# A gated attention block with a split-FP32 feed-forward: sum transfers, token loads and weight splits of chunk 0 at other places

## The reference

```python
x = x + tanh(g_xattn[0]) * wkv(time_decay, time_first, layernorm(x), ctx_2048)   # x is 16 x 256 x 512
x = x + tanh(g_ffn[0]) * ffn(layernorm(x), W1, W2, W3)

# ffn: D = 512, H = 2048
hidden = silu(x @ W1.T) * (x @ W3.T)
hidden = fwht(hidden)            # Walsh-Hadamard over H, normalised by 1/sqrt(H)
out = hidden @ W2.T
```

## Time and profile before

| | us |
|---|---|
| runs of the kernel | 1056.58 (median), 1054.04, 1057.97 |
| profiled execution | 1057.62 |
| its span, first to last instruction | 1055.8 |
| tensor engine busy | 997.6 (94%) |
| VectorE busy | 801.8 (76%) |
| ScalarE busy | 439.6 (42%) |
| GpSimd busy | 274.2 (26%) |
| first pair of chunk 1 starts at | 216.07 |
| mean granted clock of the tensor engine | 0.988 |

### The profile page before, as it was taken

One profiled execution on the slowest core, in us unless ns is written; L12 is line 12 of the kernel. 1 busy time (PEld: TensorE's weight loads), 2 busy tenths in 40 slices (PEclk: granted clock), 3 DMA queues, 4 the chain that ended last, 5 costly groups with the idle time before them and its releaser, 6 DMA issues.

```text
span 1055.8 us, 17503 instructions
## 1 busy us (share of the span) xinstructions
PE 997.6 (94%) x6988; PEld 691.6 (66%) x6988; DVE 801.8 (76%) x1288; ACT 439.6 (42%) x736; POOL 274.2 (26%) x212
## 2 busy tenths in 40 slices
PE   5799899689999999999999999999999999999998
PEld 4565344256677677776777777777777777777775
DVE  7977594989989995889769995889669994753334
ACT  6875342246243443455243542444243542522221
POOL 1344232211432033211422124221322124211111
PEclk9999999799999999999999999999999999999999
DMA  9699999694885446354745446353645433444331
GB/s 352 233 340 291 321 255 227 109 355 168 293 301 173 151 188 240 100 213 155 267 164 178 146 177 239 114 218 143 264 160 180 163 126 151 160 166 165 125 145 41
DMA packets 47042, 210.03 MB, mean 199 GB/s; under 512 B 9328, under 2 KB 26864, under 8 KB 36336
## 3 DMA queue, kind: packets, MB, share of 16 engines
q1 hardware_dynamic: 38128, 192.13, 50.2%
q0 software_dynamic: 8832, 16.78, 7.6%
HBM read 183.70 MB, written 41.97 MB: 214 GB/s over the span
## 4 chain that ended last, share of the span: by engine, by line
PE 69%; DVE 17%; DMA 6%; issue 5%; ACT 2%; SPq 0%; DVEq 0%; POOL 0%
PE pl L714 8%; PE pl L716 8%; PE pl L715 8%; PE po L726 7%; PE po L728 7%; PE pg L714 6%; PE pg L715 6%; PE pg L716 6%; PE po L737 4%; PE po L735 4%; DMA bv<-x_tok 2%; DMA wts<-up_stage 2%; DVE x L1432 2%; DVE work L1604 2%; DVE bv L1295 1%
## 5 line engine op out<-in xcount | busy, mean ns | idle before, releaser
L1759 POOL TENSOR_TENSOR work<-work 128x512 bf16<-128x512 f32 x112 | 163.9, 1464 | 595.4 <-DVE work L1604 595.4
L726 PE MATMUL po<-work,w 128*128 128x512 f16 x456 | 173.0, 379 | 2.2 <-DVE x L1432 1.3
L728 PE MATMUL po<-work,w 128*128 128x512 f16 x456 | 172.8, 379 | 0.0
L1060 ACT ACTIVATE work<-work 128x256 f32<-128x256 f32 x168 | 68.4, 415 | 210.2 <-DVE work L1511 210.1
L714 PE MATMUL pg<-wts 128*128 128x256 f16 x448 | 122.5, 273 | 4.8 <-DVE work L1511 4.7
L1511 DVE TENSOR_TENSOR work<-pl,wts 128x256 f32<-128x256 f32 x168 | 65.1, 414 | 80.1 <-PE pl L716 77.5
L715 PE MATMUL pg<-wts 128*128 128x256 bf16 x448 | 122.4, 273 | 0.0
L716 PE MATMUL pg<-wts 128*128 128x256 f16 x448 | 122.4, 273 | 0.0
L714 PE MATMUL pl<-xn,wts 128*128 128x256 f16 x448 | 122.3, 273 | 0.0
L715 PE MATMUL pl<-xn,wts 128*128 128x256 bf16 x448 | 122.2, 273 | 0.0
L716 PE MATMUL pl<-xn,wts 128*128 128x256 f16 x448 | 122.1, 273 | 0.0
(11 more groups left out here) (206 smaller groups left out, 2159.6 us busy)
## 6 DMA issues: line engine op xcount, KB each, us to landing
wts<-up_stage SPq DMA_DIRECT2D x56, 2048.0 KB, 8.0
up_stage<-wts SPq DMA_DIRECT2D x8, 1024.0 KB, 13.2
up_stage<-wts SPq DMA_DIRECT2D x16, 512.0 KB, 8.2
ev<-ctx_t SPq DMA_DIRECT2D x7, 1024.0 KB, 11.0
xin<-x_t SPq DMA_DIRECT2D x7, 1024.0 KB, 7.5
bv<-x_tok SPq DMA_DIRECT2D x7, 1024.0 KB, 10.0
out_t<-x SPq DMA_DIRECT2D x7, 1024.0 KB, 4.8
wts<-up_sums SPq DMA_DIRECT2D x11, 512.0 KB, 9.0
```

The source lines that it names most:

```text
L726: pe.matmul(po[:, d, :], w2h[:, j, d * P:d * P + P], hh[:, b, :], start=start, stop=False, skip_group_check=True)
L728: pe.matmul(po[:, d, :], w2l[:, j, d * P:d * P + P], hh[:, b, :], start=False, stop=False, skip_group_check=True)
L1060: act.activation(sg[:, slot, cols], src, ACT.Silu, scale=(1.0, -1.0)[slot]).then_inc(acted, 1)
L1759: pool.tensor_tensor(hl[:, b, :], hf[:, slot, :], hh[:, b, :], ALU.subtract).then_inc(pair_lo, 1)
```

## The change

Four things move; no instruction's work is changed and none is added or taken away.

1. GpSimd's list between W2's tiles: the first adds of group 0 and the copies of group 1 are issued behind the clamp of tile 7 instead of behind that of tile 10 and the first two low halves; the second adds of group 0 and the first adds of group 1 come in front of the clamps of tiles 11 and 12; the third adds of group 0 behind the clamp of tile 15. `STEPS_AT` places the rest, in slots 0 to 9 instead of 0 to 12.
2. Units 14 and 15 are cast and split in slots 4 and 5 instead of 12 (`unit_slot`).
3. `SUMS_AT`: sums 0 and 1 both in slot 5, 2 in slot 8, 3 and 4 in slot 10, 5 in 11, 6 in 13, 7 in 14. `next_tok` is in slot 12 instead of 11.
4. SP's list: plain pieces 4 and 5 are stored ahead of the loads of sums 0 to 2, piece 7 behind the load of sum 4; v, x and tokens of chunk 2 (counted from 0) are fetched behind the loads of sums 4 and 5.

```diff
-                sum_var=11, var=(13, 0), rsqrt=13, norm=14, next_tok=11)
-
-SUMS_AT = {4: (0,), 5: (1,), 7: (2,), 8: (3,), 10: (4,), 11: (5,), 12: (6,), 13: (7,)}
+                sum_var=11, var=(13, 0), rsqrt=13, norm=14, next_tok=12)
+
+SUMS_AT = {5: (0, 1), 8: (2,), 10: (3, 4), 11: (5,), 13: (6,), 14: (7,)}
...
-STEPS_AT = {0: ((0, "second"),), 1: ((1, "first"),), 2: ((0, "third"),), 3: ((2, "copy"),), 4: ((1, "second"),),
-            5: ((1, "third"),), 6: ((2, "first"),), 7: ((3, "copy"),), 8: ((2, "second"),), 9: ((2, "third"),),
-            10: ((3, "first"),), 11: ((3, "second"),), 12: ((3, "third"),)}
+STEPS_AT = {0: ((1, "second"),), 1: ((2, "copy"),), 2: ((1, "third"),), 3: ((2, "first"),), 4: ((3, "copy"),),
+            5: ((2, "second"),), 6: ((3, "first"),), 7: ((2, "third"),), 8: ((3, "second"),), 9: ((3, "third"),)}
...
-        unit_slot = {0: (8, 9), 1: (10, 11), 3: (12,), 4: (13,), 12: (14, 15)}
+        unit_slot = {0: (8, 9), 1: (10, 11), 3: (12,), 4: (13, 14), 5: (15,)}
...
             put_plain(3)
+            put_plain(4)
+            put_plain(5)
             for n in range(0, 3):
                 load_again(n)
-            put_plain(4)
-            put_plain(5)
+            put_plain(6)
             put_sums(0)
             load_again(3)
             put_sums(1)
-            put_plain(6)
             load_again(4)
+            put_plain(7)
+            load_v(2)
             put_sums(2)
             load_again(5)
+            load_x(2)
+            load_tokens(2)
             put_sums(3)
             load_again(6)
-            load_v(2)
             put_sums(4)
             load_again(7)
-            load_x(2)
-            load_tokens(2)
             put_sums(5)
-            put_plain(7)
             put_factors(Run(3))
...
             copy_group(0)
-            for i in range(3, 11):
+            for i in range(3, 8):
+                tile_clamp(i)
+            add_first(0)
+            copy_group(1)
+            for i in range(8, 11):
                 tile_clamp(i)
             pool.wait_ge(rows_mm, 2 * KT)
             for j in range(0, 2):
                 hidden_lo(Run(0), j)
-            add_first(0)
-            copy_group(1)
+            add_second(0)
+            add_first(1)
             for i in range(11, 13):
                 tile_clamp(i)
             for j in range(2, 4):
                 hidden_lo(Run(0), j)
             for i in range(13, TILES):
                 tile_clamp(i)
+            add_third(0)
             ffn()
```

## The result

| | before | changed kernel |
|---|---|---|
| median (lowest to highest) of 9 runs each, us | 1056.58 (1054.04 to 1059.15) | 1050.95 (1048.55 to 1052.63) |
| profiled execution, us | 1057.62 | 1049.72 |
| its span, us | 1055.8 | 1047.9 |
| tensor engine busy, us | 997.6 | 991.6 |
| mean granted clock | 0.988 | 0.992 |

The ratio of the times is 0.9945, with a 95% interval of 0.993 to 0.996: the change makes the kernel 5.6 us faster by the medians. The prediction was 1040 us, with 1035 to 1048 for the range: the sign was right, but only a third of the predicted gain of 16.3 us came, and the time lies outside the range.

A forecast was written before the change was run, and what follows sets the result against it. It took the tensor engine to bound the kernel from 400 us on, and one chain through chunk 0 before the first pair. 19.3 us less 3.0 gives 16.3, taking the median from 1056.58 to 1040 us, range 1035 to 1048.

The forecast's parts named there:

- GpSimd's queue between W2's tiles: Before tile 11's product: transfers issued 13.3 us earlier put waits for landings ahead of clamps; cost +3.0 us, range 0 to 6.
- rival E: Tiles 11 and 12: slower kernel, each microsecond the second copy lands after about 68 delays everything; 1060 at 42 us; chance 0.03.
- rival A: GpSimd's order costs more: 5 to 6 us at tile 11, some of 3 us in slots 0 to 3; 1045; chance 0.16.
- Slots 0 to 3: Group 1's second and third adds hold back low halves of hidden tiles; costed at nothing, up to 3 us without cover.
- First weight sums: VectorE's wait for the first sum goes, scan starts 5.8 us earlier; the 5.20 us wait before slot 8 vanishes.
- The new wait before slot 9: Tensor engine, before slot 9's gate product: a small new wait for silu 8 of some 2.5 us.
- Slots 9 to 13: Chunk 2's tokens land in time and units 14 and 15 are split early, so slot 14 waits for nothing: 12.5 us.
- Entry to the pairs: Before chunk 1's first pair: the ring's load lands last, at 196.8, leaving a wait of 4.4 us (3.56 before).
- 19.3 us of gain: First pair of chunk 1 starts at 196.8 instead of 216.07, before taking off 3.0 us for the start.
- Rival B: No cost at the clamps, transfers landing in 6.4 to 8.8 us: 1037.3, with the ring early 1035; chance 0.11.
- C: Sums of group 0 land later than 110; with the load landing at 115, 5.8 us not won: 1046; chance 0.10.
- D: Tokens land as late relative to their use, or another wait holds slot 14: 1052 to 1057; chance 0.05.

The follow-up runs named there:

- v later: Changed kernel with the store of plain piece 0 and the load of chunk 1's v issued behind chunk 1's tokens and plain piece 2; 1045.91 us.
- both together: Changed kernel with plain piece 0 and v behind chunk 1's tokens and plain piece 2, and sums 0 and 1 in slots 6 and 7; 1045.2 us.
- first adds behind: Changed kernel with only the first adds of group 1 moved behind the clamp of tile 15; 1054.08 us.
- the first experiment: Changed kernel with group 0's second adds and group 1's first adds behind the clamp of tile 15, later steps some slots later; 1045.57 us.
- the first two experiments: The first experiment, 1045.57 us; and the changed kernel with GpSimd's list and `STEPS_AT` of the kernel before, 1048.17 us.
- the first and seventh experiments: The first experiment, 1045.57 us; and that kernel with sums 0 and 1 in slots 6 and 7 instead of both in slot 5, 1041.77 us.

## Why the prediction was wrong, point by point

**The step that failed: GpSimd's queue between W2's tiles, +3.0 us, range 0 to 6.** It measured 11.2 us: 9.40 of waiting, 1.5 at the lower clock and 0.3 of small shifts. The mechanism was named, with the order of instructions behind it and the rule of rival E: every microsecond that the second copy lands after 68 is one for the whole kernel. With the landing measured (29.3 us after an issue at about 48, the step released at 77.6) that rule gives some 9.5 us. What failed is the number put into it. The late end of my working was 4.1 us, with a landing of 23.4 us; I took 1.1 us off for a quieter tail. The landing was 5.9 us longer, the tail brought nothing, and the clock, priced at nothing, took 1.5 us. I took 13.0 to 23.4 us from a time when the queues had other work and moved them, unchanged, to a stretch whose row had said DMA share 1.00, 350 GB/s. The room in the tail was 0.20 x 8 us = 1.6 us of all engines. In the changed kernel this stretch, 58 to 66, has a share of 1.18, and over 46 to 80 us 270 x 12 + 379 x 8 + 347 x 14 give 11.1 MB; the same windows of the trace of before (350, 214 and 378 GB/s) give 11.2 MB. So the earlier issue moved no more bytes in these 34 us, and SP's transfers landed later as GpSimd's did: I read this as sharing. That the load beside them matters was tested: with 2 MB less beside them the adds landed in 10.3 and 15.2 us instead of 15.5 and 24.4, and the slowest of the four in 20.0 instead of 29.3. That the first adds of group 1 carried most of it was tested too: without them 9.40 fell to 0.75 us, some 2 us of which is scatter of the landings.

That the upper end was 6 us, and rival A only 5 to 6 us with 0.16, is the same mistake: the bound came from the longest landing seen, not from a busier queue than the one seen.

**The clock.** I priced no lower clock at tile 11, though rows 2 had shown what an idle stretch does to it. The wait of 9.4 us brought 1.5 us more.

**Slots 0 to 3, nothing, up to 3 us.** Right for the changed kernel: no wait for low halves stands there. But the cover was the late start itself. With the start in time, 6.72 us (v later), 6.20 us (both together) and 14.82 us (first adds behind) stood at this place. "Up to 3 us" was far too low as the price without cover.

**First weight sums, 5.8 us.** Right. With 11.2 us for the start, the scan should start at 128.9 and did at 130.29; a clamp of 1.48 us (0.43 elsewhere) and a subtraction of 2.83 us (1.64 in the earlier trace rows) of VectorE just ahead of it more than account for the rest. Slot 8's wait went to 0.80 us. The new wait before slot 9, about 2.5 us, was measured as 2.80.

**Slots 9 to 13, 12.5 us.** Right: no wait for the tokens (issued 164.56, when 152.7 + 11.2 = 163.9 was expected), none before slot 14.

**Entry to the pairs.** Right in what ends last, the ring: issued at 189.63 (176.9 + 11.2 = 188.1 expected), landed 18.3 us later (19.9 taken), the first pair at 207.90 (196.8 + 11.2 = 208.0). The wait there is 2.90 us (4.4 expected).

**The sum.** 19.3 us of gain less 11.2 us gives 8.1 us; the first pair is 216.07 - 207.90 = 8.2 us earlier. The profiled executions differ by 7.9 us, since the later phase is 0.3 us longer. Against the medians it is 5.6 us: the other 2.3 us are where the two profiled executions lie in their spread.

**One reservation.** The 19.3 us and the 11.2 us are not independent. Each order that freed the start brought a wait later on: sums (7.12 us), tokens (8.71), low halves (6.72), and so won back 5.4, 0.2 and 5.0 us of the 11.2. In the first experiment two things brought the wait back: VectorE asked 11.2 us sooner, and the third adds, issued at nearly the same time, landed later, so that the load of the first sum went out 8.6 us later. Had tile 11 been on time with everything else as changed, part of the 19.3 us might not have come; no kernel here shows that case by itself.

**Rival B**, no cost at the clamps, did not happen: the adds took 15.5 and 24.4 us. The Trainium skill, page "DMA: Bandwidth & Descriptors", section "Anatomy of one DMA — SWDGE (gpsimd) path", from which 3.2 us was estimated, disagrees with the changed kernel's trace by a factor of 5 to 8, more than with the earlier trace rows, where it is 4 to 6. **Rival A** had the right mechanism at half its size, and its share in slots 0 to 3 did not come. **C**, late sums, did not happen here, but did in the first two experiments, where the start was punctual and the load of the first sum went out at 107.58 and 111.8 instead of 99.02. **D** did not happen. **E** remained what it was, a line from 68 us on, of which the kernel went through 11.2 of the 19.3 us; the line is steeper than one for one, since 9.4 us of waiting cost 10.9 with the clock.

## What to carry to other kernels

A landing time belongs to the load of its moment: before moving a transfer to an earlier stretch, look at the DMA share there, and if it is near 1.0 do not bound the landing by the longest one seen elsewhere. The share has no ceiling at 1.00 (1.18 and 1.16 stand above), so look at the rate as well. The bytes already queued would again have been too few here, by an estimate: the 6 MB issued from 45.8 to 51.8 us (four of SP, two of GpSimd) are 19 us at the 327 GB/s of 46 to 80 us. Only with the 3 MB that SP issued from 60 to 67 us, during the wait, does it come to 29 us, near the 29.3 measured. No run tests this way of reckoning. A step that waits for a landing belongs, on an engine that works in order, behind the work that others need at once; and the data it makes are better asked for a slot later, behind something that runs anyway, than hurried (the first and seventh experiments: 5.4 us, and 3.8 us by the medians with intervals that overlap). A saved wait is worth its full length only if no later wait would have absorbed it, and a new delay costs its full length only if none will: read both kernels' remaining waits before adding terms.

## What the runs showed of the hardware that was not expected

Landings depend strongly on what runs beside them, and not for the adding transfers alone. The same two adds of 512 KB, issued at the same 46.2 us, landed in 10.3 and 15.2 us or in 15.5 and 24.4 us, by 2 MB more or less on SP's queue, and SP's four transfers issued from 46.3 to 51.8 us, which landed after 8.7 to 9.7 us before, took 14.3 to 21.2 us with GpSimd's four beside them. With these in the stretch from 46 to 58 us the DMA engines were as busy as before, but the profile counts fewer bytes: share 1.04 and 270 GB/s, against 1.00 and 350. With the 2 MB taken away it was 1.03 and 246 GB/s, and the adds landed sooner all the same.

A wait of 9.40 us of the tensor engine in W2's phase left it at the lower clock for a part of what followed (0.86 over 80 to 90 us, though the engine was busy for all of the 10.00 us). The products behind it took 5.38 instead of 3.88 us, so the wait's price was 10.9 us, not 9.4.

A wait of 9.66 us at the start, 11.3 us with what followed, changed the time of the whole kernel by nothing measurable (ratio 1.0, 0.9986 to 1.0015), since two later waits took it up.
